# Expert biases loaded earlier in three groups, and experts 4 to 7 loaded on GpSimd's queue

## The reference, cut to what matters

```python
x = x + xattn(layernorm(x), ctx)        # linear attention, 16 heads, gate, Wo
x = x + ffn(layernorm(x))               # 8 experts, each token uses 2
# ffn:
logits = x @ Wr; w, sel = top_k(logits, 2); w = softmax(w)
for e in range(8):
    out = out + gate[..., e:e+1] * (x @ We[e] + be[e])
```

## Time and profile before

| what | value |
|---|---|
| median of 3 runs (lowest, highest) | 614.75 us (614.43, 615.74) |
| the profiled execution's own time | 610.47 us |
| its span, first to last instruction | 608.9 us |
| busy: PE, DVE, ACT, POOL | 552.5, 324.3, 197.8, 167.3 us |
| mean share of the DMA engines, mean rate | slices from 1 to 9 tenths, 187 GB/s |
| mean granted TensorE clock | 0.973 of full |

### The profile page before, as it was taken

One profiled execution on the slowest core, in us unless ns is written; L12 is line 12 of the kernel. 1 busy time (PEld: TensorE's weight loads), 2 busy tenths in 40 slices (PEclk: granted clock), 3 DMA queues, 4 the chain that ended last, 5 costly groups with the idle time before them and its releaser, 6 DMA issues.

```text
span 608.9 us, 12257 instructions
## 1 busy us (share of the span) xinstructions
PE 552.5 (91%) x3840; PEld 450.7 (74%) x3841; DVE 324.3 (53%) x857; ACT 197.8 (32%) x348; POOL 167.3 (27%) x195
## 2 busy tenths in 40 slices
PE   5999997999999999999999999995899999998750
PEld 4778786788778878877878887884788788776640
DVE  4553275366336636535763643773567544448643
ACT  5465422434431343444243343332111111111100
POOL 3015644313550121455030260001022000056313
PEclk9999999999998999999999999997899999999985
DMA  8713245612633051254134127869867468789946
GB/s 283 288 37 138 105 160 187 241 54 104 211 119 103 27 214 69 107 203 158 48 118 158 45 92 291 294 194 432 344 208 227 153 199 274 217 250 370 409 165 188
DMA packets 44430, 113.92 MB, mean 187 GB/s; under 512 B 4976, under 2 KB 4976, under 8 KB 43504
## 3 DMA queue, kind: packets, MB, share of 16 engines
q1 hardware_dynamic: 24240, 57.43, 27.8%
q0 software_dynamic: 11232, 39.85, 18.4%
q10 hardware_dynamic: 8928, 16.26, 7.0%
HBM read 66.86 MB, written 46.66 MB: 186 GB/s over the span
## 4 chain that ended last, share of the span: by engine, by line
PE 62%; DMA 12%; issue 5%; DVE 4%; POOL 3%; ACT 2%; POOLq 0%; DVEq 0%; ACTq 0%; SPq 0%
PE pj L1101 17%; PE pj L1103 16%; PE pj L1102 16%; PE tp L1093 4%; DMA khat<-xs 4%; DMA y<-zeros 3%; PE tp L1164 2%; PE pj L1184 2%; PE pj L1109 2%; POOL aux L535 1%; DMA wraw<-in_L_ffn_We_dram 1%; PE kvb L1156 1%; DMA qhat<-y,gidx 1%; DMA we_halves<-aux 1%; DVE qhat L930 1%
## 5 line engine op out<-in xcount | busy, mean ns | idle before, releaser
L1101 PE MATMUL pj<-R 128*128 128x512 f32 x448 | 184.9, 413 | 12.5 <-DVE R L808 12.5
L1103 PE MATMUL pj<-R 128*128 128x512 f32 x448 | 176.5, 394 | 0.0
L1102 PE MATMUL pj<-R 128*128 128x512 f32 x448 | 176.2, 393 | 0.0
L1101 PEld LDWEIGHTS pj<-R 128*128 128x128 f32 x448 | 85.0, 190 | 30.3 <-DVE R L808 12.1
L1103 PEld LDWEIGHTS pj<-R 128*128 128x128 f32 x448 | 84.8, 189 | 19.2
L1102 PEld LDWEIGHTS pj<-R 128*128 128x128 f32 x448 | 85.1, 190 | 15.2
L1101 PE MATMUL pj<-R,aux 128*128 x184 | 77.2, 419 | 5.4 <-issue 2.6
L1103 PE MATMUL pj<-R,aux 128*128 x184 | 72.7, 395 | 0.0
L1102 PE MATMUL pj<-R,aux 128*128 x184 | 72.6, 394 | 0.0
L718 ACT CAST aux<-tp 128x512 fp32r<-128x512 f32 x46 | 26.9, 585 | 118.9 <-PE tp L1164 115.1
L873 DVE SCALAR_TENSOR_TENSOR khat<-buf,khat 128x512 f32<-128x512 f32 x32 | 27.3, 854 | 58.1 <-ACT buf L677 58.0
(11 more groups left out here) (162 smaller groups left out, 697.9 us busy)
## 6 DMA issues: line engine op xcount, KB each, us to landing
we_halves<-aux POOLq DMA_DIRECT2D x14, 1024.0 KB, 5.1
R<-we_halves SPq DMA_DIRECT2D x7, 2048.0 KB, 11.6
khat<-xs SPq DMA_DIRECT2D x46, 256.0 KB
wraw<-in_L_ffn_We_dram POOLq DMA_DIRECT2D x16, 512.0 KB, 6.5
buf<-in_ctx_dram SPq DMA_DIRECT2D x15, 512.0 KB, 3.8
y<-kvbd ACTq DMA_DIRECT2D x23, 256.0 KB, 3.6
y<-zeros ACTq DMA_DIRECT2D x23, 256.0 KB
wraw<-in_x_dram SPq DMA_DIRECT2D x4, 1024.0 KB, 7.6
```

What stands on the lines that cost most here:

```text
L1101: nc.tensor.matmul(bank[:, :], s_hi(k), m_hi(k), start=(k == 0), stop=False)
L1102: nc.tensor.matmul(bank[:, :], s_hi(k), m_lo(k), start=False, stop=False)
L1103: last = nc.tensor.matmul(bank[:, :], s_lo(k), m_hi(k), start=False, stop=(k == KT - 1))
```

## The change

The eight biases go in three groups, each after the wait that frees its part of `buf`; experts 4 to 7 leave SP's queue and are issued by GpSimd: 4 after the last gate product, 5 when 4 has landed, 6 and 7 after the last O. The scratch of the first plan moves from `vones` to the second slot of `khat`.

```diff
@@ SP @@
+            def load_be(e):
+
+                sp.dma_start(be_all[:, e, :], be[e:e + 1, :].broadcast_to((P, D))).then_inc(be_loaded, 16)
+
             PAIRS = (FIRST[1] - 3) // 2
+            sp.wait_ge(SEMS["t_c"], nth("t_c", B - 1, ST - 1))
+            for e in range(4):
+                load_be(e)
             sp.wait_ge(wx_stored, 16 * 2 * (E - 1))
             sp.wait_ge(SEMS["v"], nth("v", B - 1, ST - 1))
             load_halves(1)
             load_halves(2)
+            sp.wait_ge(SEMS["kv"], nth("kv", B - 1, ST - 1))
+            load_be(4)
+            load_be(5)
             sp.wait_ge(SEMS["q"], nth("q", B - 1, G - 1))
             load_halves(3)
+            sp.wait_ge(SEMS["qhat"], nth("qhat", B - 1, G - 1))
+            load_be(6)
+            load_be(7)
             sp.wait_ge(planned, 1)
...
             load_tile(0, 0, 0)
             load_tile(0, 1, 1)
-            sp.wait_ge(SEMS["qhat"], nth("qhat", B - 1, G - 1))
-            for e in range(E):
-                sp.dma_start(be_all[:, e, :], be[e:e + 1, :].broadcast_to((P, D))).then_inc(be_loaded, 16)
-            sp.wait_ge(SEMS["g"], nth("g", B - 1, TT - 1))
-            load_halves(4)
-            load_halves(5)
             load_tile(0, 2, 0)
             sp.wait_ge(SEMS["wo"], nth("wo", B - 1, TT - 1))
             load_tile(0, 3, 1)
-            load_halves(6)
             load_tile(0, 4, 0)
-            load_halves(7)
@@ GpSimd @@
+            def load_halves(e):
+
+                pool.dma_start(R[:, 2 * e:2 * e + 2, :, :].rearrange("p a k d -> p (a k d)").bitcast(F32), wx_dram[e, :, :]).then_inc(wx_loaded[e - 1], 16)
+
             halves_in(1)
-            for t in range(TT):
-                scale(1, t, 1, "_x2", last, t)
+            scale(1, 0, 1, "_x2", last, 0)
+            pool.wait_ge(SEMS["g"], nth("g", last, TT - 1))
+            load_halves(4)
+            scale(1, 1, 1, "_x2", last, 1)
+            scale(1, 2, 1, "_x2", last, 2)
+            scale(1, 3, 1, "_x2", last, 3)
             halves_in(2)
             halves_in(3)
             halves_in(4)
+            load_halves(5)
             pool.wait_ge(SEMS["wo"], nth("wo", last, TT - 1))
+            load_halves(6)
+            load_halves(7)
             nc.gpsimd.memset(bias[:, :], 0.0).then_inc(zeroed, 1)
@@ DVE @@
-            queries(B - 1, plan(0, vones.rearrange("p s g c -> p (s g c)")))
+            queries(B - 1, plan(0, khat[:, 1, :]))
```

## The result

| | us |
|---|---|
| before, median of 4 runs (lowest, highest) | 614.90 (614.43, 615.74) |
| after, median of 4 runs (lowest, highest) | 622.95 (618.21, 624.70) |
| ratio, 95% interval | 1.0117 [1.0061, 1.0174] |
| profiled execution of after, its span | 622.96, 621.4 |
| the same ratio, measured again on another chip (12 and 23 runs) | 1.0067 [1.0040, 1.0093] |

By the two ratios the change makes the kernel slower by 4 to 7 us. The forecast was 616.0 with a range up to 618.5; the time lies above it.

What follows compares the result with a forecast made beforehand. PE was taken as the bound, busy 552.5 of 608.9 us, with time to gain only from idle waits or its clock. T(5) 1.0 us sooner and 2.2 us clock lost gave +1.2 on 614.75: 616.0 us, range 607 to 618.5.

Steps and rivals of the forecast that it cites:

- GpSimd's new wait and expert 4: GpSimd's wait for the last gate product, ending near 406.6, then expert 4's issue between scale steps: 0 us.
- tile 0's cover: Slack before T(0) at 409.65: tile 0 starts 1.5 us later, over 3 us left after a 4 us landing.
- if T(0) or T(1) has to wait for its tile: Sign at the first two tiles that would show the prediction wrong.
- Biases 0 to 3: Issued on SP after the turn at 360.66, done by 363.3, while SP would only wait: 0 us.
- the scratch: First plan's scratch at a new address: DVE runs the same instructions, 0 us.
- Biases 4 to 7: Issued ahead of the pads, tile 0 starts 1.5 us later but is covered: 0 us; 1.5 us without the cover.
- Tile 2: Lands before 416, ahead of PE's need at 417.06: gives back 6.6 us idle and 2.8 us clock, 9.4 us.
- Experts 5 to 7 and tile 5: Tile 5 waits behind GpSimd's 16 KB packets and x2r: T(5) only 1.0 us sooner, 2.2 us clock lost.
- rival A: GpSimd's packets are 4 KB, so T(5) comes 6.9 us sooner: 610.1 us, down to 607.8; chance 0.28.
- Rival C: The first queue's committed transfers go first, tile 4 lands late, T(4) starts near 435: 617 us, at most 619; chance 0.12.
- B: Small transfers pass nearly unhindered, tile 5 is hidden too, the whole 11.1 us come: 603.6 us; chance 0.10.
- D: Same megabytes must land before tile 5 and the clock loss only changes place: no effect, 614.75 us; chance 0.08.

Runs made afterwards that it cites:

- a1: The changed kernel again, unaltered, on another chip; ratio to before 1.0067 [1.0040, 1.0093].
- e2: Kernel before with GpSimd's half of the change only: experts 4 to 7 on GpSimd's queue, biases at their old place; ratio to before 1.0029.
- e5: Changed kernel, with GpSimd issuing expert 4 only when tile 1 has landed; ratio to before 1.0040.
- e1: Changed kernel with experts 4 to 7 back on SP's queue at their old places, so only the biases move; ratio to before 0.9948.
- e3: Changed kernel with each of GpSimd's expert loads cut into four transfers with runs of 4 KB; ratio to before 0.9947.
- e4: Changed kernel with x2r's 1 MB load moved behind SP's loop of tile loads; ratio to before 0.9941.
- e6: Changed kernel with both edits of e4 and e5: x2r behind the tile loop, expert 4 held until tile 1 has landed; ratio to before 0.9938.
- e8: e7 with the eight biases back in one group behind tile 1; ratio to before 0.9909.
- e9: e7 with x2r's 1 MB back between tile 4 and tile 5; ratio to before 0.9857.
- e7: Changed kernel, but experts 4 to 7 on SP's queue in 512 KB quarters between tile loads, x2r behind the tile loop; ratio to before 0.9823.
- a2: The kernel before, unchanged, profiled again on a fourth chip; ratio to itself 0.9986 [0.9949, 1.0023].
- a3: e7 run again unchanged, to test it on possibly another chip; ratio to before 0.9838 [0.9766, 0.9910].

## Why the prediction was wrong

*The failed step* is the one on GpSimd's new wait and expert 4: "The last gate product ends near 406.6". Near 406.6 is when SP **issued** expert 4 (406.50), and SP had been issuing biases until 406.45. The gate product had ended over 4 us sooner; what stands behind it on PE, and the end of GpSimd's first scale step, stand in the timelines of before:

```profile
402.15 1.11 PE L1184 MATMUL pj<-kvbd,qhat 64*128 64x66 f32 x16
```

```profile
402.38 0.19 POOL L503 TENSOR_TENSOR shift<-shift,rstd 128x1 f32<-128x1 f32 x1
```

With both over, GpSimd issued expert 4 some 3.9 us sooner than SP had, and ahead of tiles 0 and 1, which the biases had moved back by 3.2 us. The forecast checked tile 0's cover against a landing time of 4 us, and expert 4's issue against GpSimd's own work, and never set the two beside each other. It named "if T(0) or T(1) has to wait for its tile" as what would make it wrong, and priced a lost cover at 1.5 us, without a fall of the clock and without what a late T(0) does to the loads behind it.

What it cost, from KV, in after: T(0) waits 2.15 us and its stretch runs cold, 4.77 us to T(1) where before has 3.18. That moves the last scale step by 3.9 us, and with it expert 5's issue by 4.2 (49.17, forecast 44.97). In a1, where the clock stayed up behind T(0), expert 5 went out 2.3 us later than forecast. The rest of the working held but for one term that was 1.3 us too small: from expert 5's issue to T(5) the forecast has 23.2 us, and after, a1, e2 and e5 have 24.43, 24.58, 24.52 and 24.45. From T(5) to T(6) it has 2.2 us of clock lost and the trace shows 6.40 - 4.63 = 1.8. The sum: T(6) was forecast at +1.2 us and came at +6.2; 4.2 + 1.2 - 0.4 = 5.0 is the difference. e5, which removes that one overlap, gives +3.0 at T(6) and +2.4 in time.

*Biases 0 to 3, the scratch*: 0, as said; T(0) in e1 starts at 38.33, where before has 38.32. *Biases 4 to 7*: "covered" is right alone (e1) and wrong together with expert 4 (after). The delay is 3.2 us and not 1.5: the pads start 1.9 us later, their issue is 0.2 us shorter, and from its end to tile 0's issue it takes 1.6 us longer.

*Tile 2*: right. T(2) does not wait in after, nor in e5, where expert 4 went out 1.7 us later after KV than forecast. *Experts 5 to 7 and tile 5*: right in mechanism. Packets are of 16 KB, turns go by packets, and 256 KB take some 19 us. On the page of the Trainium skill "DMA: Bandwidth & Descriptors", section "SWDGE vs HWDGE vs iDMA", GpSimd's packets are preferably at most 4096 B. Here a run of 16 KB stayed one packet, so the measurement decides, and rival A, whose gain hung on it, did not come. e3 shows what A had wanted, but only with T(0)'s wait added.

*Rival C* came in part, as T(4)'s wait of 3.30 us. It cost little by itself here, since tile 5's load was issued behind T(3), before that wait. *B and D* did not occur.

*The range* ended at 618.5 because no case held a wait of T(0) beside the late tile 5. Against e5 that term was worth 3.1 us at T(6) in after and 1.9 in a1, and by the ratios 4.8 and 1.7.

## What to carry to other kernels

When a transfer moves to an engine that is free, its new time is when its condition comes true and the new engine is free, not when the old engine got to it. Find that time in the trace, and put it beside the times of the small urgent loads that used to stand ahead of it. On full DMA engines a second queue added no rate here (429 GB/s in 415 to 420 us of before, 431 in 435 to 440 of after); it takes a share by packets, so the queue with large packets wins. Large loads cut to pieces and set between the urgent ones on one queue, with the biases early, gave 9 to 11 us where the same bytes whole on a second queue lost 4 to 7.

## What the runs showed of the hardware

**A queue's first packets are late while another queue is full.** Tile 0 was issued at 406.37. The DMA queues of after, from 408 to 410 us and from 410 to 412:

```profile
q0 software_dynamic: 50, 0.82, 99.7%
```

```profile
q0 software_dynamic: 48, 0.79, 92.7%
q1 hardware_dynamic: 37, 0.08, 10.1%
```

No packet of tile 0 moved for at least 3.6 us. With no other queue at work the first packets came 0.9 to 1.4 us after the issue (e1, issue 404.56, 25 packets from 405.5 to 406; e5, issue 402.08, 22 from 403 to 403.5), so the delay is not that of an issue alone. In e3, whose packets are small, tile 0 was issued at 405.19 and had four packets by 409 (two of them by 408.5); q1 took half of the engines' time only from 410 on:

```profile
q0 software_dynamic: 171, 0.62, 84.7%
q1 hardware_dynamic: 37, 0.08, 13.0%
```

```profile
q0 software_dynamic: 114, 0.40, 48.8%
q1 hardware_dynamic: 199, 0.36, 47.1%
```

Turns by packets seem to begin only behind what the first queue has already committed. That is a reading of these stretches and was not tried by itself.

**The clock forgives short waits.** Around waits of 2.8 us and more for a tile the granted clock fell to 0.50 every time, before their end, at once or up to some 2 us later. Behind T(4) of e4, which waited 3.34 us up to 433.24 and turned at full clock, the windows (columns as in the earlier trace rows) show it late (in steps of 1 us it is 0.50 from 435 to 437):

```profile
433.00:436.00 3.00, 2.47 (x9) 1.91 (x10) 2.06 (x12) 1.08 (x3) 0.00 (x0) 0.74 1.00 419
436.00:439.00 3.00, 2.83 (x11) 2.01 (x9) 1.02 (x3) 0.08 (x1) 0.00 (x0) 0.69 1.03 431
```

Waits of 0.2 to 0.9 us cost nothing more than themselves. Near 2 us it went both ways: T(0) of after (2.15 us) had turns of 1.09 us, T(0) of e3 (2.02 us) turns of 0.63 and 3.23 us to T(1), as at full clock; T(4) of e5 (2.03 us) was followed by a fall to 0.50, T(4) of e6 (1.91 us) by none.

**A stall near the end that goes with the chip.** In after's profile PE stands still ahead of the split of tile 38, and the chain of waits has a piece that no queue explains. Its line of the chain, and DVE's and PE's of the timeline:

```profile
555.07 5.21 another core or an unknown queue
```

```profile
560.53 0.69 DVE L1033 TENSOR_TENSOR kvbd<-pj,buf 128x512 f32<-128x512 f32 x1 [5.52 <-remote]
```

```profile
562.05 0.79 PE L1117 MATMUL pj<-R,aux 128*128 x1 [4.70 <-DVE aux L828]
```

It covers the 3.6 us of the span left open above: from T(6) to the end the eight profiles with the stall take 167.2 to 169.4 us, the other six 162.4 to 164.2, and the kernels of both groups have experts on either queue. All profiles on two of the chips have it (e1 to e4; a1, e8, e9), none of those on two others (e5 to e7; a2, a3). That fits the medians of before, 616.67 and 617.28 us against 611.48 and 612.75. The chips of the first profiles of before and after are not known, and before itself was profiled only where no profile has it. What it is stays open; ratios within one chip are free of it if it meets every kernel there.
